# A fused graph-attention network on one core: the attention layers in another slot order, with V, the output projection and the low parts of keys moved

## The chip, the core and the metric

The kernel runs as one program on one core of a Trainium2 chip. The core has TensorE (PE, matrix products; its weight loads are shown as PEld), VectorE (DVE), ScalarE (ACT), GpSimd (POOL) and SyncE (SP), which issues all DMAs here. Each engine works through its own instructions in order; semaphores tie them together. The metric is the device time of one execution in microseconds (us), lower is better.

## What is computed

One graph layer (12 heads, gated) and three attention layers over 32 samples of 256 nodes with 384 features. Each layer ends in a layer norm. The change is in the attention layers only:

```python
def _L1_gnn_ref(seq_inputs, Wq, bq, Wk, bk, Wv, bv, Wf, bf, graph_mask):
    q = _heads(seq_inputs @ Wq + bq)      # 6 heads of 64
    k = _heads(seq_inputs @ Wk + bk)
    v = _heads(seq_inputs @ Wv + bv)
    scores = jnp.einsum('bhqd,bhkd->bhqk', q, k) / np.sqrt(HEAD_SIZE)
    bias = jnp.where(graph_mask, 0.0, NEG)[:, None]
    probs = jax.nn.softmax(scores + bias, axis=-1)
    ctx = jnp.einsum('bhqk,bhkd->bhqd', probs, v)
    ctx = ctx.transpose(0, 2, 1, 3).reshape(seq_inputs.shape[0], seq_inputs.shape[1], H)
    return ctx @ Wf + bf

x = _layernorm(x + _L1_gnn_ref(x, ..., adj), axis=-1)   # and so for L2, L3
```

## The kernel before

**Numbers in two parts.** Products in `float32r` are made of a high and a low part of each operand: `product` (L83 to L88) issues three matmuls, low by high, high by low and high by high. So each operand is split after it is made: ScalarE copies the high part out of the bank (`high_xt`, `high_qk`, `high_ct`), VectorE subtracts it and writes the low part (`low_xt`, `low_qk`, `low_ct`).

**Slots.** The order of work on every engine is written out by hand. The attention layers run sample by sample, 96 samples (32 in each of three layers), in slots; sample (half, u) is number 2 x half + u. In one slot, `nxt` is the sample whose x is transposed and projected, `cur` the one before it (scores, softmax) and `prev` the one before that (contexts, output projection). `every_slot_of_all_layers` calls each engine's `slot` in that order; `crossing` is the hand-written stretch in which the last sample of the graph layer and the first two of attention overlap.

**TensorE** in a slot: transposes of x (`transpose_x`, L1411), scores of heads 0 and 1, q and k of chunk 0 (`make_qk`; a chunk is 128 of 384 features, two heads), scores 2 and 3, chunk 1, contexts of `prev` (L1478), scores 4 and 5, V (`make_v`), chunk 2, output projection of `prev` (`make_back`). Three banks `pj` serve all projections in the turn of `BANK_ORDER`. The first transposes wait on `pj_read` until the last low parts of the sample before are read out of the bank.

**The stack.** For the scores, q and k of both heads of a chunk lie in `stack` with high and low parts in the two halves of the partitions. ScalarE writes one half (`own_rows`, L800), two DMAs per chunk copy the other half across partitions (`move`, L374). The low part of k lies in a tile of its own, `k_lo`, zero in the rows of the other head, and is written by two 64-row instructions (L1056).

**The way of the probabilities.** VectorE adds the mask and takes the maximum (`mask_and_max`, L1066), ScalarE the exponential (L807), VectorE the reciprocal of the sums for each pair of heads (`invert`, L1079), GpSimd multiplies (`normalise`, L579), VectorE transposes in blocks of 32 (`turn`, L1087), a DMA writes the pair to DRAM (`lay`, L381, 512 KB) and another reads it back with the blocks in place (`fetch`, L388); then TensorE makes the contexts. SyncE waits until a `lay` has landed before it issues its `fetch`. It also moves, loads the next x and adjacency (`load_again`), and stores results (`store`), all from one queue, in a fixed order.

**GpSimd** also makes the mask, adds the output bias to x (L557) and does the layer norm (L562 to L572).

## Time and profile before

| | |
|---|---|
| Median of 3 runs | 3052.48 us (3051.24 to 3055.53) |
| The profiled execution | 3051.53 us, span of the core 3049.7 us |
| Mean granted TensorE clock | 0.961 |
| Busy, share of the span | TensorE 91%, VectorE 85%, ScalarE 75%, GpSimd 59% |
| Graph layer | from the start to about 850 us |
| Attention layers | from about 850 us to the end |

A busy share is the time in which an engine had an instruction in work. Since TensorE's matmuls overlap (a row's duration is longer than the distance to the next start), starts are the better measure of its pace. The granted clock is a share of full speed, which is 2.4 GHz; the other level is 1.2 GHz. The waits of a DMA queue are SyncE's own waits before it can issue.

### The profile page before, as it was taken

To read this page: it belongs to the slowest core of one execution; us is meant where nothing else is said; L and a number is where in the kernel's file an instruction comes from. 1 tells how busy PE (TensorE), PEld (TensorE's weight loads), DVE (VectorE), ACT (ScalarE), POOL (GpSimd) and SP (SyncE) were. 2 spreads that over 40 slices of the span, in tenths; PEclk is the share of its full clock that TensorE was granted. 3 is DMA by queue.
4 is the path that set the end of the run, shared out by engine and by line. 5 is a ranking of instruction groups with operands and counts; after the bars stand their busy time and mean duration, and the time that the engine had idled before them with its cause. 6 is when DMAs were issued, how large, how long until landed. Compare 5 with 4: busy or idle time off the path is not lost. (4 is left out here: it accounts for less than half of the span.)

```text
span 3049.7 us, 67047 instructions
## 1 busy us (share of the span) xinstructions
PE 2771.7 (91%) x20128; PEld 2479.0 (81%) x20128; DVE 2587.4 (85%) x7497; ACT 2272.8 (75%) x6600; POOL 1809.7 (59%) x1550
## 2 busy tenths in 40 slices
PE   8999999999988899899898899899899898998996
PEld 7888888888877888888888888788888888888885
DVE  6999998998888888888888888888888888888885
ACT  7999999999966667666666666676666676666663
POOL 3777766666655566555555566555555555555554
PEclk9999999999999999999999999999999999999998
DMA  2111111111166666666667666666666666666664
GB/s 88 35 35 35 35 35 35 35 35 35 50 199 226 211 208 215 210 217 209 211 213 235 212 216 209 219 206 220 208 212 212 207 216 209 216 208 208 219 205 155
DMA packets 346726, 500.45 MB, mean 164 GB/s; under 512 B 58112, under 2 KB 272000, under 8 KB 345984
## 3 DMA queue, kind: packets, MB, share of 16 engines
q1 hardware_dynamic: 346368, 496.16, 50.2%
q8 instruction: 165, 2.70, 0.4%
q14 instruction: 193, 1.58, 0.2%
HBM read 219.24 MB, written 201.33 MB: 138 GB/s over the span
## 5 line engine op out<-in xcount | busy, mean ns | idle before, releaser
L579 POOL TENSOR_TENSOR probs<-probs,recs 128x1024 f32<-128x1024 f32 x288 | 545.5, 1894 | 461.7 <-DVE recs L1079 461.7
L1087 DVE STREAM_TRANSPOSE turned_sb<-probs 128x512 f32<-128x512 f32 x576 | 609.8, 1099 | 205.2 <-POOL probs L579 202.3
L807 ACT ACTIVATE probs<-logits,nmax 128x256 f32<-128x256 f32 x1152 | 572.4, 498 | 173.0 <-DVE nmax L1066 170.6
L86 PE MATMUL pj<-xt_hi,w_lo 128*128 128x256 f32 x1728 | 506.6, 293 | 12.6 <-issue 11.1
L87 PE MATMUL pj<-xt_lo,w_hi 128*128 128x256 f32 x1728 | 500.2, 289 | 0.0
L88 PE MATMUL pj<-xt_hi,w_hi 128*128 128x256 f32 x1728 | 498.1, 288 | 0.0
L1066 DVE CUSTOM_DVE_ANT_0 logits<-s,mask 128x256 f32<-128x256 f32 x1152 | 423.8, 420 | 73.5 <-PE s L1466 63.4
L557 POOL TENSOR_TENSOR residual<-x,br 128x384 f32<-128x384 f32 x192 | 190.0, 1011 | 426.7 <-DVE mix L1098 426.7
L678 ACT ACTIVATE g_exps<-g_v,g_nmax 128x256 f32<-128x256 f32 x768 | 385.2, 515 | 2.9 <-DVE g_nmax L972 0.6
L800 ACT ACTIVATE stack<-split 64x512 fp32r<-64x512 f32 x576 | 363.4, 631 | 12.4
L86 PEld LDWEIGHTS pj<-xt_hi,w_lo 128*128 128x128 f32 x1728 | 349.7, 202 | 20.3 <-issue 18.2
L785 ACT ACTIVATE xt_hi<-pj 128x384 fp32r<-128x384 f32 x192 | 94.4, 491 | 357.4 <-PE pj L1411 357.2
L792 ACT ACTIVATE split<-pj,bc 128x256 fp32r<-128x256 f32 x576 | 238.1, 464 | 164.0 <-PE pj L88 163.8
L87 PEld LDWEIGHTS pj<-xt_lo,w_hi 128*128 128x128 f32 x1728 | 345.1, 200 | 0.0
L1465 PE MATMUL s<-k_lo,stack 128*128 128x256 f32 x1152 | 341.6, 323 | 3.5 <-DVE nmax L1066 3.5
L88 PEld LDWEIGHTS pj<-xt_hi,w_hi 128*128 128x128 f32 x1728 | 342.5, 198 | 0.0
L572 POOL TENSOR_SCALAR out<-mix,mv,rstd 128x384 f32<-128x384 f32 x192 | 316.0, 1652 | 20.0 <-issue 19.4
L1466 PE MATMUL s<-stack 128*128 128x256 f32 x1152 | 324.1, 308 | 0.0
L972 DVE CUSTOM_DVE_ANT_0 g_v<-s,g_v 128x256 f32<-128x256 f32 x768 | 286.9, 420 | 35.9 <-ACT g_v L672 29.9
L1411 PE MATMUL pj<-identity,x 128*128 128x128 f32 x576 | 114.9, 316 | 202.3 <-DVE k_lo L1056 191.7
L1056 DVE SCALAR_TENSOR_TENSOR k_lo<-pj,bc,split 64x256 fp32r<-64x256 f32 x576 | 275.9, 479 | 4.1
L1465 PEld LDWEIGHTS s<-k_lo,stack 128*128 128x128 f32 x1152 | 245.0, 213 | 40.3 <-issue 36.5
(119 smaller groups left out, 7726.5 us busy)
## 6 DMA issues: line engine op xcount, KB each, us to landing
turned<-turned_sb SPq DMA_DIRECT2D x288, 512.0 KB, 4.0
pt_copy<-turned SPq DMA_DIRECT2D x288, 512.0 KB, 4.3
stack<-split SPq DMA_DIRECT2D x576, 128.0 KB, 2.6
y<-out SPq DMA_DIRECT2D x128, 384.0 KB, 4.7
x<-y SPq DMA_DIRECT2D x96, 384.0 KB, 4.2
x<-x SPq DMA_DIRECT2D x32, 384.0 KB, 3.1
adj<-adj SPq DMA_DIRECT2D x128, 64.0 KB, 4.1
w_whole<-att_w SPq DMA_DIRECT2D x3, 2304.0 KB, 11.4
```

Of the source, the lines that this page charges most:

```text
L86: pe.matmul(out, a[1], b[0], start=first, stop=False)
L87: pe.matmul(out, a[0], b[1], start=False, stop=False)
L88: return pe.matmul(out, a[0], b[0], start=False, stop=last)
L572: pool.tensor_scalar(out_sb[u][:, t, :], mix[:, t, :], mv[:, t, 0:1], rstd[:, t:t + 1], ALU.subtract, ALU.mult).then_inc(ln_done, 1)
L579: pool.tensor_tensor(probs[:, heads, :, :].rearrange("p h t n -> p (h t) n"), probs[:, heads, :, :].rearrange("p h t n -> p (h t) n"), rec ...
L678: last = act.activation(g_exps[:, h % 4, t, :], g_v_sb[:, h % 3, t, :], ACT.Exp, scale=-1.0, bias=g_nmax[:, u, h, t:t + 1], accum_out=g_su ...
L800: last = act.activation(stack[rows_of(s), c, s, :, :], f32(split_slot(u, c)[rows_of(s), K_HI:Q_HI + 1:2, :]), ACT.Identity)
L807: last = act.activation(probs[:, (HEADS * u + h) % 4, t, :], logits[:, h % 2, t, :], ACT.Exp, scale=-1.0, bias=nmax[:, u, h, t:t + 1], acc ...
L1066: last = dve.tensor_tensor_reduce(out=logits[:, h % 2, t, :], in0=s_ps[h % 2][:, t, :], in1=mask[u][:, t, :], scale=-HEAD_DIM ** -0.5, sca ...
L1087: last = dve.transpose(turned_sb[b][:, :, :].rearrange("p k (z h q) -> p k z h q", z=NT, h=2 * NT)[:, :, kt], probs[:, 2 * b:2 * b + 2, :, ...
L1465: pe.matmul(s_ps[s][:, t, :], queries, k_lo[:, c, s, :], start=True, stop=False)
L1466: last = pe.matmul(s_ps[s][:, t, :], queries, stack[:, c, s, STACK_K, :], start=False, stop=True)
```

## The change

The slots are called with up to four samples: `new` (transposes of x, q and k), `cur` (scores, softmax, and now V), `prev` (contexts) and `old` (now the output projection, residual, statistics and norm); SyncE also gets the one before `old`, whose result it stores. So V and the output projection come one slot later than before. The contexts move from the middle to the end of TensorE's slot. The third pair of `cur` is normalised, transposed, written and fetched in the slot after. Scores are issued head by head instead of in pairs, and each waits for the maximum two heads before.

The low part of k goes into the same tile as the others (`split`, now four wide) in one 128-row instruction, and ScalarE's copy (`own_rows`) takes it to the stack, which is three wide now; `k_lo` is gone. That copy now waits for the low parts (`pj_read`) instead of the high ones. The moves across partitions take q low and k high, two runs of 1 KB a row that no longer lie side by side in the source.

The banks are taken in another turn, and the waits of `make_v`, `make_back`, `make_qk` follow it. `crossing` is adapted (V of the second sample and the third transpose of the first fall into the slots). The diff, cut to its core; a line of "..." also stands where removed lines of the old slots, printed above, are left out:

```diff
...
+def every_slot_of_all_layers(slot, behind=3):
+
+
+    def sample(i):
+        return divmod(i, 2) if 0 <= i < LAYERS * B else None
+
+    for i in range(2, LAYERS * B + behind):
+        slot(*(sample(i - k) for k in range(behind + 1)))
...
-        stack = sb("stack", [P, DC, 2, 2, N], F32R)
-        k_lo = sb("k_lo", [P, DC, 2, N], F32R)
+        stack = sb("stack", [P, DC, 2, 3, N], F32R)
...
-        BANK_ORDER = ("x0", "x1", "qk0", "qk1", "v0", "v1", "qk2", "back0", "back1")
+        BANK_ORDER = ("v0", "x0", "v1", "x1", "back0", "back1", "qk0", "qk1", "qk2")
...
-        K_HI, Q_LO, Q_HI = range(3)
+        Q_LO, Q_HI, K_HI, K_LO = range(4)
...
-                    sp.dma_start(f32(stack[rows_of(1 - s), c, s, :, :]), f32(split_slot(u, c)[rows_of(s), K_HI:Q_LO + 1, :])).then_inc(moved[c], 16)
+                    sp.dma_start(f32(stack[rows_of(1 - s), c, s, STACK_Q:STACK_K + 1, :]), f32(split_slot(u, c)[rows_of(s), Q_LO:K_HI + 1:2, :])).then_inc(moved[c], 16)
...
+            def slot(new, cur, prev, old, stored):
+                if cur:
+                    move(*cur, 2)
+                if prev:
+                    fetch(*prev, 0)
+                    lay(*prev, 1)
+                    fetch(*prev, 1)
+                if stored:
+                    store(*stored)
+                elif prev == first:
+                    g_store(*g_odd)
+                if prev:
+                    lay(*prev, 2)
+                    fetch(*prev, 2)
+                if new:
+                    move(*new, 0)
+                if cur:
+                    load_again(*cur)
                     lay(*cur, 0)
...
+                if new:
+                    move(*new, 1)
...
+            def slot(new, cur, prev, old):
+                if prev:
+                    normalise(*prev, 2)
                 if cur:
                     normalise(*cur, 0)
                 if old:
                     inverse_std(*old, EPS)
+                if cur:
+                    add_output_bias(*cur, layer_of(cur[0]))
+                    normalise(*cur, 1)
+                if new:
+                    make_mask(*new, prev)
+                if old:
                     layer_norm(*old)
...
+                if new:
+                    part = 2 * (new[0] % HALVES) + new[1] - 8
+                    if 0 <= part < PARTS and layer_of(new[0]) + 1 < LAYERS:
+                        split_weights(layer_of(new[0]) + 1, part)
...
             def own_rows(half, u, c):
-                act.wait_ge(pj_hi, split_of(half, u, QK[c]))
+                act.wait_ge(pj_read, split_of(half, u, QK[c]))
                 act.wait_ge(scores, scored(half, u, c))
                 for s in range(2):
-                    last = act.activation(stack[rows_of(s), c, s, :, :], f32(split_slot(u, c)[rows_of(s), K_HI:Q_HI + 1:2, :]), ACT.Identity)
+                    last = act.activation(stack[rows_of(s), c, s, :, :], f32(split_slot(u, c)[rows_of(s), Q_HI:K_LO + 1, :]), ACT.Identity)
                 last.then_inc(owned, 1)
...
+            def slot(new, cur, prev, old):
+                if old:
+                    high_ct(*old, 1, layer_of(old[0]))
+                    high_ct(*old, 2, layer_of(old[0]))
+                if cur:
+                    own_rows(*cur, 1)
+                if new:
+                    high_xt(*new, 0)
+                if cur:
+                    copy_v(*cur, 0)
                     exp(*cur, 0)
+                    copy_v(*cur, 1)
                     exp(*cur, 1)
...
+                if new:
+                    high_xt(*new, 1)
+                if cur:
+                    own_rows(*cur, 2)
                     exp(*cur, 2)
+                if new:
+                    high_qk(*new, 0, layer_of(new[0]))
+                if cur:
                     exp(*cur, 3)
...
+                if new:
+                    own_rows(*new, 0)
+                    high_qk(*new, 1, layer_of(new[0]))
                 if cur:
                     exp(*cur, 4)
+                if new:
+                    high_qk(*new, 2, layer_of(new[0]))
+                if prev:
+                    high_ct(*prev, 0, layer_of(prev[0]))
+                if cur:
                     exp(*cur, 5)
...
             def low_qk(half, u, c, layer):
                 dve.wait_ge(pj_hi, split_of(half, u, QK[c]))
-                dve.wait_ge(scores, scored(half, u, c))
-                parts, ps = split_slot(u, c), bank(half, f"qk{c}")
-                dve.scalar_tensor_tensor(parts[:, Q_LO, :], ps[:, Q * N:(Q + 1) * N], bc[:, layer, Q, c:c + 1], f32(parts[:, Q_HI, :]), ALU.add, ALU.subtract)
-                for s in range(2):
-                    rows = rows_of(s)
-                    last = dve.scalar_tensor_tensor(k_lo[rows, c, s, :], ps[rows, K * N:(K + 1) * N], bc[rows, layer, K, c:c + 1],
-                                                    f32(parts[rows, K_HI, :]), ALU.add, ALU.subtract)
+                parts, ps = split_slot(u, c), bank(half, u, f"qk{c}")
+                for m, hi, lo in ((Q, Q_HI, Q_LO), (K, K_HI, K_LO)):
+                    last = dve.scalar_tensor_tensor(parts[:, lo, :], ps[:, m * N:(m + 1) * N], bc[:, layer, m, c:c + 1], f32(parts[:, hi, :]), ALU.add, ALU.subtract)
                 last.then_inc(pj_read, 1)
...
+            def slot(new, cur, prev, old):
+                if old:
+                    low_ct(*old, 1, layer_of(old[0]))
+                if cur:
+                    mask_and_max(*cur, 0)
+                if old:
+                    low_ct(*old, 2, layer_of(old[0]))
+                if new:
+                    low_xt(*new, 0)
+                if cur:
+                    mask_and_max(*cur, 1)
+                if prev:
+                    turn(*prev, 2)
+                if new:
+                    low_xt(*new, 1)
+                if cur:
+                    mask_and_max(*cur, 2)
+                    invert(*cur, 0)
+                if old:
+                    add_back(*old, 0)
+                if cur:
+                    mask_and_max(*cur, 3)
                 if old:
                     add_back(*old, 1)
...
                     statistics(*old)
...
+                if new:
+                    low_qk(*new, 0, layer_of(new[0]))
+                if cur:
+                    invert(*cur, 1)
+                    mask_and_max(*cur, 4)
                     turn(*cur, 0)
...
+                if new:
+                    low_qk(*new, 1, layer_of(new[0]))
+                if cur:
                     mask_and_max(*cur, 5)
...
                     turn(*cur, 1)
+                if new:
+                    low_qk(*new, 2, layer_of(new[0]))
+                if prev:
+                    low_ct(*prev, 0, layer_of(prev[0]))
+                if cur:
                     invert(*cur, 2)
...
+            def transpose_x(half, u, t):
+                if (half, u) == second:
+                    pe.wait_ge(v_read, at(NT, *first, NT))
+                    pe.wait_ge(pj_read, split_of(*first, QK[2]))
+                elif t == 0:
+                    pe.wait_ge(pj_read, split_of(half, u, QK[1]) - HI_STEPS)
+                elif half:
+                    pe.wait_ge(v_read, at(NT, half, u, 1 - NT))
...
+            def scores_of(half, u, h):
+
+                c, s = divmod(h, 2)
+                pe.wait_ge(maxed, at(HEADS, half, u, h - 1))
+                if s == 0:
+                    pe.wait_ge(pj_read, split_of(half, u, QK[c]))
+                    pe.wait_ge(owned, at(DC, half, u, c + 1))
+                    pe.wait_ge(moved[c], moves_of(half, u))
+                for t in range(NT):
+                    queries = stack[:, c, s, STACK_Q, t * P:(t + 1) * P]
+                    pe.matmul(s_ps[s][:, t, :], queries, stack[:, c, s, STACK_K_LO, :], start=True, stop=False)
+                    last = pe.matmul(s_ps[s][:, t, :], queries, stack[:, c, s, STACK_K, :], start=False, stop=True)
+                last.then_inc(scores, 1)
...
+            def slot(new, cur, prev, old):
+                if cur:
+                    scores_of(*cur, 0)
+                    make_v(*cur, 0, layer_of(cur[0]))
+                if new:
+                    transpose_x(*new, 0)
+                if cur:
+                    scores_of(*cur, 1)
+                    make_v(*cur, 1, layer_of(cur[0]))
+                    scores_of(*cur, 2)
+                if new:
+                    transpose_x(*new, 1)
+                if old:
+                    make_back(*old, 0, new, cur, layer_of(old[0]))
+                if cur:
+                    scores_of(*cur, 3)
+                if old:
+                    make_back(*old, 1, new, cur, layer_of(old[0]))
+                if new:
+                    make_qk(*new, 0, layer_of(new[0]))
+                if cur:
+                    scores_of(*cur, 4)
+                if new:
+                    make_qk(*new, 1, layer_of(new[0]))
+                if cur:
+                    scores_of(*cur, 5)
+                if new:
+                    make_qk(*new, 2, layer_of(new[0]))
+                if prev:
+                    for c in range(DC):
+                        pair_of_contexts(*prev, c)
```

SyncE, one slot in the middle of the attention layers. `turned` is the tile in DRAM, so a row `turned<-turned_sb` is a `lay` and `pt_copy<-turned` a `fetch`; `laid` and `fetched` count their landings. Before:

```order
L381 DMA turned<-turned_sb 128x1024 [waits turned,fetched0]
L374 DMA stack<-split 64x512 [waits pj_read,scores]
L374 DMA stack<-split 64x512
L388 DMA pt_copy<-turned 128x4x256 [waits laid0,contexts]
L355 DMA y<-out 128x2x384 [waits ln_done]
L381 DMA turned<-turned_sb 128x1024 [waits turned,fetched1]
L388 DMA pt_copy<-turned 128x4x256 [waits laid1,contexts]
L381 DMA turned<-turned_sb 128x1024 [waits turned,fetched2]
L374 DMA stack<-split 64x512 [waits pj_read,scores]
L374 DMA stack<-split 64x512
L388 DMA pt_copy<-turned 128x4x256 [waits laid0,contexts]
```

After:

```order
L373 DMA turned<-turned_sb 128x1024 [waits turned,fetched0]
L366 DMA stack<-split 64x2x256 [waits pj_read,scores]
L366 DMA stack<-split 64x2x256
L366 DMA stack<-split 64x2x256 [waits pj_read,scores]
L366 DMA stack<-split 64x2x256
L380 DMA pt_copy<-turned 128x4x256 [waits laid0,contexts]
L373 DMA turned<-turned_sb 128x1024 [waits turned,fetched1]
L380 DMA pt_copy<-turned 128x4x256 [waits laid1,contexts]
L344 DMA y<-out 128x2x384 [waits ln_done]
L373 DMA turned<-turned_sb 128x1024 [waits turned,fetched2]
L380 DMA pt_copy<-turned 128x4x256 [waits laid0,contexts]
```

Write 1 stood behind the store and now stands right behind fetch 0; the store has gone between fetch 1 and write 2. Two moves fill the time between write 0 and fetch 0, and none that between write 2 and fetch 2.

TensorE, from the end of one slot into the next. Before:

```order
L88 MATMUL pj<-w_hi,ct_hi 128x384
L1411 MATMUL pj<-identity,x 128x128 [waits x_loaded1,pj_read]
L1411 MATMUL pj<-identity,x 128x128 x2
L1411 MATMUL pj<-identity,x 128x128 [waits back_read,pj_read]
L1411 MATMUL pj<-identity,x 128x128 x2
L1465 MATMUL s<-k_lo,stack 128x256 [waits owned,moved0,pj_read,maxed]
L1466 MATMUL s<-stack 128x256
```

After, with the contexts last and the first V product behind the first head's scores:

```order
L1452 MATMUL pt<-pt_copy,v 64x256 [waits v_read,fetched1,ct_split]
L1452 MATMUL pt<-pt_copy,v 64x256 x3
L1452 MATMUL pt<-pt_copy,v 64x256 [waits v_read,fetched2,ct_split]
L1452 MATMUL pt<-pt_copy,v 64x256 x3
L1439 MATMUL s<-stack 128x256 [waits owned,moved0,pj_read,maxed]
L1440 MATMUL s<-stack 128x256
L1439 MATMUL s<-stack 128x256
L1440 MATMUL s<-stack 128x256
L76 MATMUL pj<-w_hi,xt_lo 128x384 [waits pj_read]
```

The slot began with the transposes, waiting on `pj_read`; it begins with scores now, and its last waits are those for the three fetches.

VectorE, the end of a slot and the start of the next. Before:

```order
L1087 STREAM_TRANSPOSE turned_sb<-probs 128x4x128 [waits laid1,normed]
L1087 STREAM_TRANSPOSE turned_sb<-probs 128x4x128
L1079 RECIPROCAL recs<-sums 128x4 [waits exped]
L1087 STREAM_TRANSPOSE turned_sb<-probs 128x4x128 [waits laid0,normed]
L1087 STREAM_TRANSPOSE turned_sb<-probs 128x4x128
L1053 SCALAR_TENSOR_TENSOR split<-pj,bc,split 128x256 [waits scores,pj_hi]
L1056 SCALAR_TENSOR_TENSOR k_lo<-pj,bc,split 64x256 x2
L1098 TENSOR_TENSOR mix<-pj,residual 128x384 [waits back_made,ln_done,x_biased] x2
```

After:

```order
L1056 STREAM_TRANSPOSE turned_sb<-probs 128x4x128 [waits laid0,normed]
L1056 STREAM_TRANSPOSE turned_sb<-probs 128x4x128
L1026 SCALAR_TENSOR_TENSOR split<-pj,bc,split 128x256 [waits pj_hi]
L1026 SCALAR_TENSOR_TENSOR split<-pj,bc,split 128x256
L1042 SCALAR_TENSOR_TENSOR ct_lo<-cx,bc,ct_hi 128x256 [waits ct_hi_done]
L1048 RECIPROCAL recs<-sums 128x4 [waits exped]
L1042 SCALAR_TENSOR_TENSOR ct_lo<-pt,bc,ct_hi 128x256 [waits ct_hi_done]
L1035 ISA logits,nmax<-s,mask 128x256 [waits exped,mask_ready,scores]
```

The third transpose (with its wait on `normed`) stood ahead of the last low parts of q and k; now the last low parts follow the second transpose, and the third comes in the next slot.

## Rows read from the trace of the kernel before

**Rows 1.** The page's first part: busy time and share of the span of each engine

```profile
PE 2771.7 (91%) x20128; PEld 2479.0 (81%) x20128; DVE 2587.4 (85%) x7497; ACT 2272.8 (75%) x6600; POOL 1809.7 (59%) x1550
```

**Rows 2.** Stretches: start:end, us, busy time by engine (instructions), clock, DMA share, GB/s

```profile
300.00:600.00 300.00, 293.62 (x2344) 253.82 (x2345) 271.12 (x891) 295.99 (x917) 209.94 (x197) 1.00 0.11 36
1200.00:2900.00 1700.00, 1532.42 (x10756) 1392.81 (x10755) 1441.62 (x3960) 1144.10 (x3211) 955.98 (x779) 0.95 0.66 213
```

**Rows 3.** Timeline of TensorE: start, duration, line, tiles, count, idle before; two slots' starts

```profile
856.33 1.08 PE L1411 MATMUL pj<-identity,x 128*128 128x128 f32 x4 [5.36 <-DVE k_lo L1056]
...
2979.32 0.55 PE L1411 MATMUL pj<-identity,x 128*128 128x128 f32 x3 [2.02 <-DVE k_lo L1056]
```

**Rows 4.** Waits from 1200 to 2900 us: us in all, times, longest

```profile
PE pj L1411 <- DVE k_lo L1056: 150.4, 75, 2.3
```

**Rows 5.** The same columns as rows 2, for three neighbouring slots

```profile
1204.40:1226.55 22.15, 19.73 (x145) 17.79 (x145) 19.25 (x54) 15.24 (x43) 14.02 (x12) 1.00 0.67 217
1226.55:1249.53 22.98, 20.96 (x145) 19.08 (x145) 19.35 (x54) 15.36 (x43) 14.00 (x12) 0.93 0.62 207
1249.53:1272.69 23.16, 21.01 (x144) 19.24 (x144) 19.34 (x54) 15.36 (x43) 14.00 (x12) 0.93 0.64 208
```

**Rows 6.** Timeline of TensorE in the slot that opens at 1204.40 us

```profile
1206.82 0.35 PE L86 MATMUL pj<-xt_hi,w_lo 128*128 128x256 f32 x1 [0.28 <-issue]
...
1224.19 0.34 PE L88 MATMUL pj<-w_hi,ct_hi 128*128 128x384 f32 x1
```

**Rows 7.** Timeline of VectorE near the end of a slot

```profile
1516.91 0.13 DVE L1079 RECIPROCAL recs<-sums 128x4 f32<-128x4 f32 x1
1519.16 2.08 DVE L1087 STREAM_TRANSPOSE turned_sb<-probs 128x512 f32<-128x512 f32 x2 [2.11 <-POOL probs L579]
...
1521.49 0.97 DVE L1056 SCALAR_TENSOR_TENSOR k_lo<-pj,bc,split 64x256 fp32r<-64x256 f32 x2
```

**Rows 8.** Groups by line and form over the whole span: count, busy us, mean ns

```profile
L800 ACT ACTIVATE stack<-split 64x512 fp32r<-64x512 f32 x576 | 363.4, 631 | 12.4
...
L1056 DVE SCALAR_TENSOR_TENSOR k_lo<-pj,bc,split 64x256 fp32r<-64x256 f32 x576 | 275.9, 479 | 4.1
...
L1053 DVE SCALAR_TENSOR_TENSOR split<-pj,bc,split 128x256 fp32r<-128x256 f32 x288 | 136.0, 472 | 5.0 <-ACT split L792 2.0
...
L708 ACT ACTIVATE g_ce<-g_ce 128x768 f32<-128x768 f32 x32 | 27.1, 846 | 1.4 <-DVE g_ce L951 1.4
```

**Rows 9.** Timeline of TensorE in the slot that opens at 1204.40 us: pace of its parts

```profile
1212.19 1.08 PE L1478 MATMUL cx<-pt_copy,v 128*64 128x256 f32 x8
...
1214.93 0.39 PE L1465 MATMUL s<-k_lo,stack 128*128 128x256 f32 x1
...
1219.10 0.28 PE L86 MATMUL pj<-xt_hi,w_lo 128*128 128x256 f32 x1
...
1221.22 0.34 PE L86 MATMUL pj<-w_hi,ct_lo 128*128 128x384 f32 x1
```

**Rows 10.** SyncE's own waits from 1200 to 2900 us

```profile
SPq L81 <- DMA turned<-turned_sb: 523.7, 193, 5.1
```

**Rows 11.** Timeline of SyncE's DMA issues: start, duration of the issue, line

```profile
1517.08 0.33 SPq L381 DMA_DIRECT2D turned<-turned_sb  x1
1521.09 0.36 SPq L388 DMA_DIRECT2D pt_copy<-turned  x1
1521.56 0.44 SPq L381 DMA_DIRECT2D turned<-turned_sb  x1
1522.63 1.18 SPq L374 DMA_DIRECT2D stack<-split  x2
1527.08 0.37 SPq L388 DMA_DIRECT2D pt_copy<-turned  x1
1527.56 0.44 SPq L350 DMA_DIRECT2D x<-y  x1
```

**Rows 12.** Landing times of the writes to DRAM (line 381), 1200 to 2900 us

```profile
DMA to landing us min/median/max: 2.6/4.0/7.7
```

More of the change, by code:

```diff
@@ L50, in g_every_slot, with layer_of @@
         slot((pair + 1, 0), (pair + 1, 1), (pair, 1))
[L53 to L75 removed]
+def every_slot_of_all_layers(slot, behind=3):
[3 more added lines that the diff above has]
+        slot(*(sample(i - k) for k in range(behind + 1)))
+def layer_of(half):
+    return half // HALVES
 def held(eng, sem, value, passed):
@@ L427, in _, with crossing @@
+                if new:
+                    move(*new, 1)
+                if new and new[1] and new[0] % HALVES == 2 and layer_of(new[0]) + 1 < LAYERS:
+                    load_weights(layer_of(new[0]) + 1)
+            def crossing():
+                for c in range(DC):
+                    move(*first, c)
+                load_again(*first)
+                g_store(*g_even)
+                move(*second, 0)
+                lay(*first, 0)
+                move(*second, 1)
             start(sp, *g_stored, *stored, *moved, *laid, *fetched)
@@ L460, in _ @@
             load(*second)
-            for layer in range(LAYERS):
-                samples_of_layer(layer)
-            end = LAYERS * HALVES - 1
-            lay(end, 1, 0)
-            fetch(end, 1, 0)
-            store(end - 1, HALVES - 2, 1)
-            lay(end, 1, 1)
-            fetch(end, 1, 1)
-            lay(end, 1, 2)
-            fetch(end, 1, 2)
-            store(end, HALVES - 1, 0)
-            store(end, HALVES - 1, 1)
+            crossing()
+            every_slot_of_all_layers(slot, behind=4)
             for u in range(2):
@@ L590, in split_weights @@
                 pool.tensor_tensor(lo, whole, f32(hi), ALU.subtract).then_inc(w_split, 1)
-            def slot(cur, nxt, prev, layers, opening=False, part=None):
-                old = before(prev)
+            def slot(new, cur, prev, old):
+                if prev:
+                    normalise(*prev, 2)
                 if cur:
@@ L630, in crossing @@
                 g_total(*g_odd)
-                normalise(*first, 2)
                 g_inverse_std(*g_odd, 4 * EPS)
@@ L651, in _ @@
             crossing()
-            every_slot_of_all_layers(pool, slot)
-            close(end_sample)
+            every_slot_of_all_layers(slot)
         @block.scalar
@@ L1106, in statistics @@
                     dve.bn_aggr(mv[:, t, :], stats[:, t, :]).then_inc(aggr, 1)
-            def slot(cur, nxt, prev, layers, opening=False, part=None):
-                _, nxt_layer, prev_layer = layers
-                old = before(prev)
+            def slot(new, cur, prev, old):
[20 more added lines that the diff above has]
+                    mask_and_max(*cur, 3)
@@ L1206, in crossing @@
                 low_qk(*second, 2, 0)
-                turn(*first, 2)
                 g_statistics(*g_odd)
@@ L1229, in _ @@
             crossing()
-            every_slot_of_all_layers(dve, slot)
-            close(end_sample)
+            every_slot_of_all_layers(slot)
         @block.tensor
```

271 lines of the change are left out of this document (62 added, 209 removed).

## Prediction

> **What bounds the kernel now.** Start with the page's first part (the span is 3049.7 us): TensorE busy 91%, VectorE 85%, ScalarE 75% [rows 1]. The medians over the span mix two stages, so the next view is the table by stretch. From 300 to 600 us (layer 0) TensorE is busy 97.9% at granted clock 1.00; from 1200 to 2900 us (the attention layers) it is busy 90% at 0.95, and the DMA share is 0.66 instead of 0.11 [rows 2]. The change touches the second stage only, so the question is how long one slot of it lasts. The six transposes of x open every slot: those of sample 2 start at 856.33 us, those of sample 95 at 2979.32 [rows 3]. That is 93 slots in 2122.99 us, 22.83 us each.
>
> Next, the waits of that stage. TensorE waits before those transposes, 75 times, 150.4 us in all, 2.0 us each, for the last low part of k (`k_lo`) [rows 4]. Three neighbouring slots show what one is made of [rows 5]: 22.15 us at clock 1.00, 22.98 and 23.16 us at 0.93. All three have the same 2.0 us wait, so a slot at full clock saves 0.8 to 1.0 us. In the first, which opens at 1204.40, the last matmul starts at 1224.19 and lasts 0.34 [rows 6]: 20.13 us. Of that, 0.28 is a stall before the q and k products [rows 6]. **TensorE's own work in a slot at full clock is thus about 19.85 us**, and the wait, the slow stretches and small stalls make up the other 3.0 of 22.83.
>
> Why is `k_lo` late? VectorE's own rows tell it [rows 7]: reciprocal at 1516.91, then 2.11 us idle for GpSimd's normalised probabilities, the transpose of the third pair (1519.16), and only then the low part of q and that of k (1521.49 to 1522.46), which TensorE waits for. VectorE waits for GpSimd, and TensorE waits for both.
>
> **The parts of the change.**
> *The low parts of k.* 288 instructions of 64x256 at 479 ns twice per chunk become one of 128x256; the q one of that shape takes 472 ns [rows 8]. VectorE saves 3 x 479 ns, 1.4 us a slot. It is busy 19.2 to 19.35 us of a slot [rows 5], so about 17.9 after. ScalarE's copy of own rows grows from 512 to 768 elements: 631 ns now; a 128x768 of layer 0 takes 846 [rows 8]. Bounds +0 (the width hidden by the overlap of neighbours) and +0.215; I take the upper, 6 x 0.215 = 1.3 us a slot. ScalarE goes from 15.3 to 16.6 us and stays below TensorE. The copy now waits for the low part as well; behind it are the next q, k copy and an exponential. TensorE's work is unchanged.
>
> *Third transpose in the next slot.* `turn(prev, 2)` goes behind the next slot's second maximum. GpSimd gets a whole slot start for its 1.9 us, so the 2.1 us idle goes. The next transposes of x no longer wait for the last low part but for the one of chunk 1, made some 4 us earlier. **The 2.0 us wait goes.** V, now one slot later, waits for the banks of chunks 0 and 2; the second of these is needed 2.9 us into the slot.
>
> *What is late next on the engines.* I lay the new slot out by starts of the full-clock slot [rows 9]: contexts 2.74 us, two scores and both V products 4.17 (so a score 0.5, a V product 1.56), a q, k chunk 2.12; a back product is as long as a V product, three transposes 0.45. TensorE's start at 0: score 0 and V to 2.1, x0 2.5, score 1 and V to 4.6, score 2 and x1 5.5, back 0 to 7.1, score 3 and back 1 to 9.2, qk0 to 11.4, score 4 and qk1 to 14.1, score 5 and qk2 to 16.8, contexts to 19.6, and with the changes between kinds of product 19.85. VectorE gets the x0 copy at 3.3, then maximum 1, third transpose to about 7.0, x1, maximum 2, back 0, maximum 3, back 1 (to 10.1), statistics to 11.5, qk0's low parts from 12.5 when ScalarE has its high parts, and from there without a wait 0.9 + 0.15 + 0.7 + 2.1 + 0.9 + 0.7 + 2.1 + 0.9 = 8.45 us to the last low parts at 20.95, which is 1.1 into the next slot. TensorE's waits are met with 1 us and more to spare: x1's low part at 7.6 for 9.2, chunk 2's at 1.1 for 3.0. The engines alone would give about 19.85 us a slot.
>
> *The DMA queue.* Every pair of heads goes out to DRAM and back, and SyncE waits for the write before it issues the read: 523.7 us of waits in 75 slots, 7 us a slot, its longest [rows 10]. Before, only write 2 stood right behind a fetch, with a move in its wait. After, the order is fetch 0, write 1, fetch 1, store, write 2, fetch 2, move, load, write 0, two moves. I price that ring from SyncE's starts [rows 11], from one fetch 2 to the next. Fetch 2 to the move 0.5, the move 1.2, x and adjacency 1.0, then write 0. A write issued alone comes back after 4.0 (1517.08 to 1521.09); one issued 0.5 us behind a fetch needs 5.5 (1521.56 to 1527.08), because its data queue behind the fetch's. Write 0 stands behind the load: between them, 5.0. Fetch 0 and the issue of write 1: 0.5. Write 1 stands right behind a fetch: 5.5. Fetch 1 and store: 1.05. Write 2 stands behind a fetch and a 384 KB store: 6.0. Sum 0.5 + 1.2 + 1.0 + 5.0 + 0.5 + 5.5 + 1.05 + 6.0 = **20.75 us a slot.** That is above the engines' 19.85: the wait removed comes back as one of about 1 us before the third pair's contexts (or at the q, k copy that waits for the move of chunk 0). Bounds of the three writes: all at the median of 4.0 [rows 12] gives 16.25 for the ring, which hides it behind TensorE (19.85); 5.5, 6.3 and 6.8 give 22.85. I keep the middle, since two of the writes stand where the 5.5 one stood.
> The moves carry the same bytes in runs of 1 KB instead of 2 KB: no row prices that; the DMA share of 0.66 [rows 2] on 22.8 us is 15 us of work, so even 1 us more leaves it below 20.7. Between 0 and +0.5 on the ring; I take 0.
>
> *Fill and drain.* The last sample still has three pairs written and fetched one after another; from 2979.32 to the end is 70.4 us. One more slot stands in the loop, but it is only back and norm, which `close` did. I take 0, bounds -5 and +5.
>
> **Sum.** 94 full slots x (22.83 - 20.75) = 195 us. The profiled execution took 3051.53 us, 0.95 below the median of 3052.48: 3051.5 - 195 = 2856. I say **2855 us.**
>
> **The rivals.**
> *A. TensorE alone.* The writes land near their median because bursts interleave better; the ring hides and a slot is 19.85. 94 x 2.98 = 280: about 2771. For it: clock 1.00 throughout layer 0 at 97.9% busy [rows 2] and the spare time above. Against it: the 5.5 us of a write behind a fetch.
> *B. The clock still falls.* The ring's wait of 1 us, or several shorter ones, keeps part of every slot at 1.2 GHz. In the rows a slow slot costs 0.8 to 1.0 us over a full-clock one [rows 5]; on top of 20.75 that is up to 21.7: 94 x 1.13 = 106, about 2945. For it: two slots in three fall now with a wait of 2.0 us. Against: in layer 0, with TensorE idle 2% of the time in many small pieces, it stays at 1.00 [rows 2]. The Trainium skill, TensorE: Matmul & The Clock Gate, section "A second HAM failure mode: psum-queue depth-cycling", says that idle moments between groups of matmuls, as a kernel cycles through its banks, can make the clock oscillate and cost throughput; the new order cuts TensorE's slot into sixteen pieces on three banks. By that rule this case is likelier; layer 0's clock [rows 2] disagrees.
> *C. Slower: the write queue saturates.* Place: writes 1 and 2 in the ring. If a write behind fetch and store lands after 7.7 us, the longest seen [rows 12], and so do all three, the ring is 20.75 + 2.7 + 2.2 + 1.7 = 27.35 and the kernel 94 x 4.5 = 425 us slower (3475); it decides from where the three together take over 18.6 us instead of 16.5. Just past it, say 8% over, is more likely than the full price. Against it: 5.5 was measured with two moves behind it as well.
> *D. Nothing.* The order view shows the waits moved as the diff says, so that TensorE's 2 us wait stays can only be if GpSimd's norm (3.3 us) at the slot's end holds up the third normalise by over 2 us; then 3050. Little speaks for it: GpSimd is busy 956 of 1700 us [rows 2].
>
> **How the numbers follow.** Forecast (ring, 20.2 to 21.2 us a slot, 2810 to 2905 us): 0.48. A: 0.25. B: 0.15. C: 0.07. D and small losses: 0.05. The range reaches down to A with a fill 5 us shorter and the stalls between products gone (19.6 a slot, 24 us), 2745, and up to B's end, 2945; C, D and the tails are left out. A measurement of this kernel can tell about 0.2% (6 us). Faster by more than that 0.89, within 0.03, slower 0.08.
>
> **What would show it.** Right: slots near 20.7 us; the wait for `k_lo` before the transposes of x gone; VectorE's instructions down by 288; SyncE's waits for the write above 7 us a slot, writes landing after 5 to 6 us, and the one TensorE wait of some size before the contexts (line 1452 of the new kernel), ended by a DMA or told as "issue". Wrong by A: no such wait, slots of 19.85, clock 1.00. Wrong by B: clock 0.93 in slots without a long wait. Wrong by C: median landing of `turned` near 7 us and a slot over 22.8. A wait of VectorE for ScalarE's copies above 1 us a slot would say that my layout of the engines was too kind.

## The result: 3030.7 us, a gain of 0.75% where 6.5% was forecast

The changed kernel takes 3030.69 us, median of 4 runs (3026.23 to 3033.22); the kernel before 3052.61 (3051.24 to 3055.53). The ratio is 0.9925 [0.9908, 0.9943]. The forecast was 2855, its range 2745 to 2945: the direction was right, the size was not, and the time lies outside the range. The profiled execution took 3031.44 us, its span is 3029.7.

**What went as said.** The page of the changed kernel, its first part, one group of part 5 and one of part 6:

```profile
PE 2752.4 (91%) x20128; PEld 2457.8 (81%) x20128; DVE 2437.9 (80%) x7209; ACT 2362.9 (78%) x6600; POOL 1805.6 (60%) x1550
...
L772 ACT ACTIVATE stack<-split 64x768 fp32r<-64x768 f32 x576 | 485.8, 843 | 3.4
...
turned<-turned_sb SPq DMA_DIRECT2D x288, 512.0 KB, 5.2
pt_copy<-turned SPq DMA_DIRECT2D x288, 512.0 KB, 4.5
stack<-split SPq DMA_DIRECT2D x576, 128.0 KB, 4.4
```

VectorE has 288 instructions fewer than in [rows 1], ScalarE's copy takes 843 ns (846 had been taken from a row of the same width, [rows 8]), and a write lands after a median of 5.2 us.

**What did not.** The waits of the changed kernel from 1200 to 2900 us (engine, line, releaser: us in all, times, longest), the engines' and then SyncE's own:

```profile
ACT split L764 <- issue: 320.8, 75, 9.0
DVE split L1026 <- ACT split L764: 254.0, 130, 4.8
...
PE pt L1452 <- issue: 145.6, 76, 5.9
```

```profile
SPq L71 <- DMA turned<-turned_sb: 762.6, 151, 9.5
SPq L71 <- DVE split L1026: 176.5, 75, 3.0
```

The wait for `k_lo` [rows 4] is gone. In its place TensorE waits 1.9 us a slot before the third pair's contexts (145.6 in 76), and two waits are there that the sum did not have: ScalarE 4.3 us a slot before its copies of q and k ("issue" means that the profile shows nothing that ended the wait), VectorE 3.4 us behind it.

The slots, by the first transposes of x of samples 2 and 95, in TensorE's timeline:

```profile
856.86 0.84 PE L1377 MATMUL pj<-identity,x 128*128 128x128 f32 x3
...
2956.87 0.61 PE L1377 MATMUL pj<-identity,x 128*128 128x128 f32 x3
```

That is 93 slots in 2100.01 us, 22.58 each, against 22.83 in [rows 3]: 23 us less, of which the tail gives back 2.4 (72.8 us from sample 95 to the end, 70.4 before). The forecast had 20.75 a slot. So 1.83 us a slot are to be explained. The attention stretch and four neighbouring slots (the columns of [rows 2]):

```profile
1200.00:2900.00 1700.00, 1531.76 (x10862) 1390.11 (x10862) 1337.92 (x3775) 1226.62 (x3248) 959.43 (x784) 0.96 0.70 215
...
1290.76:1312.64 21.88, 19.67 (x146) 17.65 (x144) 16.62 (x46) 15.12 (x40) 12.46 (x10) 1.00 0.67 207
1312.64:1336.60 23.96, 20.84 (x145) 18.74 (x145) 18.42 (x54) 16.92 (x46) 12.45 (x10) 0.93 0.66 208
1336.60:1357.55 20.95, 19.65 (x146) 17.62 (x145) 17.01 (x48) 15.59 (x42) 12.46 (x10) 1.00 0.70 221
1357.55:1380.48 22.93, 20.83 (x145) 18.91 (x145) 18.34 (x54) 16.85 (x46) 12.46 (x10) 0.93 0.70 214
```

The clock still falls (1.00 or 0.93), and the long slots are those at 0.93. That looks like rival B. It is tested below.

### The profile page after: what moved, and what is told of

Its sections match the earlier page's. It is cut to its first block and busy times, and to the rows that moved or that the text cites. A ratio compares the mean times of both kernels' runs of the same rounds, so it can differ in the third digit from the quotient of the medians.

```text
span 3029.7 us, 66563 instructions
## 1 busy us (share of the span) xinstructions
PE 2752.4 (91%) x20128; PEld 2457.8 (81%) x20128; DVE 2437.9 (80%) x7209; ACT 2362.9 (78%) x6600; POOL 1805.6 (60%) x1550
## 5 line engine op out<-in xcount | busy, mean ns | idle before, releaser
L1026 DVE SCALAR_TENSOR_TENSOR split<-pj,bc,split 128x256 fp32r<-128x256 f32 x576 | 248.3, 473 | 321.4 <-ACT split L764 318.8
L772 ACT ACTIVATE stack<-split 64x768 fp32r<-64x768 f32 x576 | 485.8, 843 | 3.4
L76 PE MATMUL pj<-xt_hi,w_lo 128*128 128x256 f32 x1728 | 483.3, 280 | 3.1 <-DVE xt_lo L1020 3.1
L77 PE MATMUL pj<-xt_lo,w_hi 128*128 128x256 f32 x1728 | 482.3, 279 | 0.0
L1452 PE MATMUL pt<-pt_copy,v 128*64 128x256 f32 x1536 | 220.3, 409 | 195.9 <-issue 193.8
L1439 PE MATMUL s<-stack 128*128 128x256 f32 x1152 | 332.2, 309 | 29.4 <-DMA stack<-split 26.2
L1452 PEld LDWEIGHTS pt<-pt_copy,v 128*64 128x64 f32 x1536 | 114.8, 143 | 277.1 <-issue 239.4
L76 PEld LDWEIGHTS pj<-xt_hi,w_lo 128*128 128x128 f32 x1728 | 325.2, 188 | 3.7 <-issue 3.7
L77 PEld LDWEIGHTS pj<-xt_lo,w_hi 128*128 128x128 f32 x1728 | 325.8, 189 | 0.0
L1440 PE MATMUL s<-stack 128*128 128x256 f32 x1152 | 312.1, 291 | 0.0
L1439 PEld LDWEIGHTS s<-stack 128*128 128x128 f32 x1152 | 226.5, 197 | 90.1 <-issue 87.7
L1440 PEld LDWEIGHTS s<-stack 128*128 128x128 f32 x1152 | 229.7, 199 | 0.0
```

Of the source, the lines that this page charges most:

```text
L76: pe.matmul(out, a[1], b[0], start=first, stop=False)
L77: pe.matmul(out, a[0], b[1], start=False, stop=False)
L772: last = act.activation(stack[rows_of(s), c, s, :, :], f32(split_slot(u, c)[rows_of(s), Q_HI:K_LO + 1, :]), ACT.Identity)
L1439: pe.matmul(s_ps[s][:, t, :], queries, stack[:, c, s, STACK_K_LO, :], start=True, stop=False)
L1440: last = pe.matmul(s_ps[s][:, t, :], queries, stack[:, c, s, STACK_K, :], start=False, stop=True)
L1452: last = pe.matmul(cx_banks[c][rows_of(s), :], v_sb[u][:, kt, h * HEAD_DIM:(h + 1) * HEAD_DIM], tokens(pt_sb[:, c, :, run]), start=kt == 0 ...
```

## Where the ring was priced too low

SyncE's starts in one slot of the changed kernel (366 is `move`, 373 `lay`, 380 `fetch`, 344 `store`):

```profile
1503.08 0.36 SPq L380 DMA_DIRECT2D pt_copy<-turned  x1
1503.62 1.25 SPq L366 DMA_DIRECT2D stack<-split  x2
1504.99 0.53 SPq L339 DMA_DIRECT2D x<-y  x1
...
1506.22 0.40 SPq L373 DMA_DIRECT2D turned<-turned_sb  x1
1506.82 5.73 SPq L366 DMA_DIRECT2D stack<-split  x4
1512.68 0.51 SPq L380 DMA_DIRECT2D pt_copy<-turned  x1
1513.31 0.47 SPq L373 DMA_DIRECT2D turned<-turned_sb  x1
1518.42 0.36 SPq L380 DMA_DIRECT2D pt_copy<-turned  x1
...
1519.44 0.40 SPq L373 DMA_DIRECT2D turned<-turned_sb  x1
1525.11 0.36 SPq L380 DMA_DIRECT2D pt_copy<-turned  x1
```

The order is the forecast's. From one start to the next, as means over 64 slots between 1200 and 2900 us with just this pattern of issues:

| piece | priced | measured |
|---|---|---|
| fetch 2 to move 0, move 0, x and adjacency to write 0 | 0.5 + 1.2 + 1.0 | 0.55 + 1.39 + 1.22 |
| **write 0 to fetch 0** | **5.0** | **0.61 + 5.84 = 6.45** |
| fetch 0 to write 1 | 0.5 | 0.64 |
| write 1 to fetch 1 | 5.5 | 5.15 |
| fetch 1 and store to write 2 | 1.05 | 1.06 |
| write 2 to fetch 2 | 6.0 | 6.00 |
| sum | 20.75 | 22.47 |

The writes behind a fetch were priced well. One piece is off by 1.45 us, and not by its landing: from issue to landing write 0 takes 5.2 us on the mean from 1200 to 2900 us, against 5.0 priced (all three writes 5.2 + 5.1 + 5.9 = 16.3, priced 16.5). The other 1.2 us is SyncE held up behind it: fetch 0 does not stand behind write 0 alone. Between them stand the moves of chunks 1 and 2 (the row of 5.73 us), and the move of chunk 2 waits for that chunk's low parts. ScalarE's and VectorE's timelines at the same time say why these are late:

```profile
1509.39 0.84 ACT L764 ACTIVATE split<-pj,bc 128x256 fp32r<-128x256 f32 x2 [4.89 <-issue]
```

```profile
1510.26 0.88 DVE L1026 SCALAR_TENSOR_TENSOR split<-pj,bc,split 128x256 fp32r<-128x256 f32 x2 [3.50 <-ACT split L764]
```

`split` has two buffers, and chunk 2 uses that of chunk 0. So `high_qk` of chunk 2 waits until the move of chunk 0 has landed (line 761). That move is issued 0.54 us behind fetch 2; ScalarE goes on 5.77 us after its issue. The second half of the move lands at 1509.32 us in the trace, and ScalarE starts at 1509.39. This closes a loop over ScalarE, VectorE and SyncE's queue, which makes the slot's length by itself: fetch 2 to move 0 0.54, to ScalarE's copy 5.77, to fetch 0 3.29 (high parts, low parts 1510.26 to 1511.14, the two moves), to write 1 0.63, to fetch 1 5.11, to write 2 1.02, to fetch 2 5.67: 22.03 us, the distance from 1503.08 to 1525.11. **Theory Q** is that this loop sets the slot. Rivals: **B** (**K** in the expectations), the fallen clock costs time of its own; **L**, the moves' runs of 1 KB land later than those of 2 KB; **S**, ScalarE's wider and later copy of own rows is what holds up its q, k copy.

## Experiments

All ratios compare with the kernel before, run beside them on the same chip (medians of 3052.6 to 3060.6 us), so gains between two runs of the table are taken from the ratios.

| | median us | ratio to before |
|---|---|---|
| changed kernel | 3030.69 | 0.9925 [0.9908, 0.9943] |
| e1, move of chunk 2 later | 2900.92 | 0.9476 [0.946, 0.9492] |
| e2, move of chunk 0 earlier | 2835.48 | 0.9268 [0.9252, 0.9285] |
| e3, both | 2812.18 | 0.919 [0.9176, 0.9204] |
| e7, both and the store moved | 2792.64 | 0.9152 [0.9126, 0.9178] |
| e4, runs of 2 KB | 3031.34 | 0.9912 [0.9898, 0.9927] |
| e5, old low parts | 3064.12 | 1.0035 [1.0018, 1.0051] |
| e6, e3 with old low parts | 2839.82 | 0.9298 [0.928, 0.9317] |
| b1, before with new low parts | 3335.42 | 1.0921 [1.09, 1.0942] |
| e8, long filler | 3266.16 | 1.0688 [1.067, 1.0706] |
| e9, shorter filler | 3053.85 | 0.9978 [0.9965, 0.9992] |

### e1: the move of chunk 2 no longer ahead of fetch 0

```diff
                 if prev:
                     fetch(*prev, 0)
                     lay(*prev, 1)
+                if cur:
+                    move(*cur, 2)
+                if prev:
                     fetch(*prev, 1)
```

(The move's lines ahead of fetch 0 are gone.)

> The changed kernel with one edit in SyncE's order: the move of chunk 2 stands behind fetch 0 and write 1 instead of ahead of fetch 0. Theory Q (the queue's ring is held by the move of chunk 2, which waits for the last low parts; write 0 to fetch 0 takes 6.45 us, of which the landing needs about 4.8): that piece falls to 4.8, the ring from 22.5 to about 20.9 us a slot, the kernel to about 2875. Rival L (the landings themselves are long, because the moves go in 1 KB runs): the bytes and runs are the same, so the slot falls by less than 0.3 us, above 3000. Rival K (TensorE's clock): the 3.5 us stretches at half clock stay, above 2980.

2900.92 us, 4.5% less than the changed kernel. The distance of write 0 and fetch 0 falls from 6.45 to 5.35 us (4.8 were expected; it is now the landing of write 0, still 5.2), write 1 to fetch 1 from 5.15 to 5.13 with the move in its wait, and the ring from 22.47 to 21.12 (20.9 expected). The granted clock is 1.00 from 1200 to 2700 us. ScalarE still waits 257.8 us in 79 slots, but SyncE's wait for VectorE's low parts, 176.5 us in the changed kernel, is gone:

```profile
SPq L71 <- DVE split L1027: 0.9, 3, 0.3
```

### e2: the move of chunk 0 ahead of fetch 2

```diff
                     lay(*prev, 2)
+                if new:
+                    move(*new, 0)
+                if prev:
                     fetch(*prev, 2)
-                if new:
-                    move(*new, 0)
```

> The changed kernel with one edit in SyncE's order: the move of chunk 0 of the new sample stands between write 2 and fetch 2 (in the wait for that write's landing) instead of behind fetch 2. Theory Q: the move's 1.4 us of issue leave the ring, it lands some 3 us earlier, so ScalarE's copy of chunk 2, the last low parts and the move of chunk 2 come earlier too and write 0 to fetch 0 falls from 6.45 to about 5. Ring 22.5 - 1.4 - 1.4 = 19.7, so TensorE's 19.85 and small waits bound it: 20.2 us a slot, about 2805. Rival L: less than 0.3 us a slot, above 3000. Rival K: above 2980.

2835.48 us (about 2805 were expected), the turn of the queue 20.25 us. Part 6 of its page, and ScalarE's wait for the moves from 1200 to 2900 us:

```profile
stack<-split SPq DMA_DIRECT2D x576, 128.0 KB, 3.0
...
ACT split L765 <- issue: 8.6, 8, 3.7
```

The moves land after a median of 3.0 us instead of 4.4 (those of chunk 0 alone, first and second: 2.6 and 2.8 instead of 4.3 and 4.8), and ScalarE's wait for them falls from 320.8 us to 8.6. The loop is cut at another place, with no byte less and no instruction less, and the gain is 6.6%, 201 us. Not all of it is the loop's: of the 2.2 us that the queue's turn loses, 1.0 is write 0 to fetch 0 (6.45 to 5.5), and some 1.4 is the issue of the two moves, which now lies in the wait for write 2; 0.2 comes back elsewhere. Two different edits that open the same loop both shorten that piece: theory Q holds.

### e3 and e7: both, and the store out of write 2's way

e3 has both edits. e7 moves the store from ahead of write 2 to behind write 0 as well:

```diff
-                if stored:
-                    store(*stored)
...
                 if prev:
                     lay(*prev, 2)
...
                     lay(*cur, 0)
+                if stored:
+                    store(*stored)
                 if new:
                     move(*new, 1)
```

> Both edits of SyncE's order. Theory Q: TensorE's own 19.85 us bound the slot already with the second edit alone, so this is 19.9 to 20.2 us a slot, 2775 to 2805, and within 1% of the second edit alone. If each edit took away a wait of its own, the two gains would add up to more. Rival L: above 3000. Rival K: above 2950.

> Both edits of the queue's order, and the store of the result from between fetch 1 and write 2 to behind write 0. Theory Q: write 2's landing loses the 384 KB ahead of it, fetch 2 is issued about 1 us earlier, and TensorE's 0.8 us wait before the third contexts goes: slot 20.0 to about 19.4 to 19.7, 2765 to 2800. Rival T (TensorE's own work bounds already): no change from 2812, within 0.3%.

2812.18 and 2792.64 us, both beat both kernels; e3 is above its 2775 to 2805 but within 1% of e2, e7 within its 2765 to 2800, with a longer slot than the 19.4 to 19.7 expected. From e3 to e7 the turn of the queue falls from 20.07 to 19.86 us: the store's 0.7 between fetch 1 and write 2 now lies in write 0's wait, and 0.5 comes back as longer waits for writes 1 and 2. In e7 the first transposes of samples 2 and 95 stand at

```profile
858.37 0.84 PE L1379 MATMUL pj<-identity,x 128*128 128x128 f32 x3
...
2721.46 0.49 PE L1379 MATMUL pj<-identity,x 128*128 128x128 f32 x3
```

20.03 us a slot, the median of the queue's turns being 19.7. The engines-alone layout of the prediction gave 19.85. Its stretch from 1200 to 2900 us and the waits in it:

```profile
1200.00:2900.00 1700.00, 1516.24 (x11254) 1391.44 (x11250) 1379.50 (x3922) 1276.88 (x3359) 1004.56 (x819) 0.99 0.68 225
```

```profile
DVE split L1028 <- ACT split L766: 83.4, 78, 1.1
...
PE pt L1454 <- issue: 54.3, 81, 4.6
```

The span ends at 2791.4 us, so the last 109 us of this stretch are empty. Up to 2700 us TensorE is busy 1449.35 us of 1500 at clock 1.00, so the slot is now near TensorE's own work. VectorE's wait is down from 3.4 to 1.1 us a slot, TensorE's from 1.9 to 0.7.

### e4: the moves in runs of 2 KB

`split` is made five wide, so that k high and q low lie side by side again; nothing else changes.

```diff
-        Q_LO, Q_HI, K_HI, K_LO = range(4)
+        K_HI, Q_LO, Q_HI, _, K_LO = range(5)
```

> The changed kernel with the tile of split parts five wide, in an order in which k high and q low lie side by side, so that each move goes in runs of 2 KB again as in the kernel before; the order of everything stays. Rival L (1 KB runs make the landings of the moves 4.4 instead of 2.6 us and hold the ring): landings of the moves back near 3, 1.4 us a slot less, about 2900. Theory Q (the moves land late because a fetch and a load are in front of them and beside them): at most 0.3 us a slot, 3003 to 3035. Rival K: no change.

3031.34 us, moves landing after a median of 4.5 us instead of 4.4: rival L falls. The "0, at most 0.5 us" of the prediction for that was 0.

### e5 and e6: the low parts as before

Two 64-row instructions write k's low part straight into the stack, ScalarE copies 512 elements, and VectorE waits again for the scores of the sample before ahead of them (that line is left out below). e5 does it in the changed kernel, e6 in e3.

```diff
-                for m, hi, lo in ((Q, Q_HI, Q_LO), (K, K_HI, K_LO)):
-                    last = dve.scalar_tensor_tensor(parts[:, lo, :], ...)
+                dve.scalar_tensor_tensor(parts[:, Q_LO, :], ...)
+                for s in range(2):
+                    last = dve.scalar_tensor_tensor(stack[rows_of(s), c, s, STACK_K_LO, :], ...)
```

> The changed kernel with the low parts of k made as before: two 64-row instructions that write the stack directly, and ScalarE's copy of own rows 512 wide. Everything else, the queue's order too, stays. Theory Q: the low parts of chunk 2 are a link of the loop move 0, ScalarE, VectorE, move 2, fetch 0; the link grows by 0.5 us, so the slot does: about 3075. Rival S (ScalarE's wider copies, +0.2 us each, six a slot, are what ate the gain): 1.3 us a slot less, about 2910.

> Both edits of the queue's order and the low parts of k as before. Where the queue no longer bounds, VectorE has 1.4 us a slot more, 19.4 instead of 17.9, beside TensorE's 19.85. Theory Q: the new instruction is worth little while VectorE has spare time; the slot grows by 0 to 0.6 us over both edits alone (2812): 2812 to 2870. Rival S: it falls, below 2800.

3064.12 and 2839.82 us. Without the wide copy, ScalarE's wait stays (308.9 us in 75 slots in e5): rival S falls. In both orders the new low parts are worth 1.1% (0.9925 against 1.0035, 0.919 against 0.9298), some 0.36 us a slot, of the 1.4 us that they take off VectorE.

### b1: the low parts alone, in the old order

The kernel before with the new `split`, the three-wide stack and the copy that waits for the low parts; order and banks as before.

> The kernel before with only the low parts of k as in the change (one 128-row instruction a chunk, own rows 768 wide and waiting for the low parts, moves in 1 KB runs), in the old order of slots. VectorE has 1.4 us a slot less, of it 0.5 directly ahead of TensorE's 2.0 us wait; if nothing else moved, 0.5 us a slot, about 3005. Against it ScalarE, which made its copy right behind the high parts, now waits for VectorE twice a slot with exponentials behind it (2 us at chunk 0, more at chunk 1). I expect that this wins: slot 24 to 25.5 us, 3150 to 3300. Rival: the copy's wait is hidden, 2990 to 3050.

3335.42 us, 9.2% slower, more than the 3150 to 3300 expected. Its waits from 1200 to 2900 us, and the three copies of one slot in ScalarE's timeline:

```profile
ACT stack L799 <- DVE split L1053: 478.4, 198, 4.2
```

```profile
1503.31 1.69 ACT L799 ACTIVATE stack<-split 64x768 fp32r<-64x768 f32 x2 [4.12 <-DVE split L1053]
...
1514.00 1.70 ACT L799 ACTIVATE stack<-split 64x768 fp32r<-64x768 f32 x2 [2.27 <-DVE split L1053]
...
1519.47 1.70 ACT L799 ACTIVATE stack<-split 64x768 fp32r<-64x768 f32 x2 [0.94 <-DVE split L1053]
```

The copy, and the exponentials behind it, now wait for VectorE at every chunk, 7.2 us in each of the 66 slots. The longest of the three is that of chunk 2: its low parts stand behind VectorE's third transpose, which waits for GpSimd. The same edit gains 1.1% in the new order.

### e8 and e9: matmuls in TensorE's idle time

Extra products (v by v, overwritten by the contexts) ahead of the wait for the third pair's fetch. e8 has 14 in one half of the bank's rows, e9 has 8 that alternate between the halves:

```diff
                 pe.wait_ge(v_read, at(NT, half, u, NT))
+                if c == DC - 1:
+                    for i in range(8):
+                        pe.matmul(cx_banks[c][rows_of(i % 2), :], v_sb[u][:, 0, 0:HEAD_DIM], v_sb[u][:, 1, 0:N], start=True, stop=True)
                 pe.wait_ge(fetched[c], fetches(half, u))
```

> The changed kernel with 14 extra matmuls (v by v, 256 columns, some 0.13 us apart, 1.9 us) that TensorE makes before it waits for the third pair's fetch; the contexts overwrite their result. It fills the idle time of about 2 us there and changes nothing that SyncE, ScalarE or VectorE wait for, so the granted clock should stay at 1.00. In seven neighbouring slots of the changed kernel the three at full clock last 20.95 to 21.88 us (mean 21.5), the four at 0.93 last 22.93 to 23.96 (23.4). If the fallen clock is a cause of its own (the loss is loop plus clock), all slots become 21.5: 93 x (22.6 - 21.5) = 100 us less, about 2930. If the clock only follows the wait and the queue's loop sets every slot, the time stays within 0.5% of 3030. If the filler itself stands in the way where no wait is, it is up to 1.9 us a slot slower in some slots, and over 3030.

3266.16 us. It doesn't tell the theories apart: the filler was mis-sized. A row of it reads

```profile
1502.87 5.99 PE L1449 MATMUL pt<-v 128*64 128x256 f32 x27
```

It took 6 us instead of 1.9 (a product shows as two records), and TensorE was busy for the whole 1700 us.

> As the run with the filler before, where each of the 14 matmuls took 0.43 us (6 us in all, more than the idle time, so that TensorE itself set a slot of 25.1 us), but with 8 matmuls that alternate between the two halves of the bank's rows, as the contexts do, whose 4 take 1.08 us: some 2.1 us. The idle time before the third pair's contexts is 2.5 us in the changed kernel. If the fallen clock is a cause of its own, about 2930 (slots of 21.5 us, as the full-clock ones of the changed kernel); if it only follows the wait and the queue's loop sets every slot, within 0.5% of 3030; a mixture lies between. Slots where the fetch has landed early are up to 2 us longer, which would work against the first.

3053.85 us, 0.5% more than the changed kernel in the ratios. The stretch and a slot's filler:

```profile
1200.00:2900.00 1700.00, 1609.67 (x11973) 1422.73 (x11970) 1330.82 (x3743) 1218.97 (x3221) 955.18 (x780) 0.99 0.70 213
```

```profile
1516.63 1.90 PE L1449 MATMUL pt<-v 128*64 128x256 f32 x16
1519.71 1.08 PE L1455 MATMUL pt<-pt_copy,v 128*64 128x256 f32 x8 [1.18 <-DMA pt_copy<-turned]
```

The clock is at 0.99, and the ring is 22.64 us as before. **With the clock back, nothing is won; so the fallen clock is a companion of the long wait and not a cause of the time.** The filler itself does not hide a gain: in 62 of the 75 slots the third contexts still start within 0.1 us of the landing of their fetch, and in the other 13 it holds them up by 12 us in all, 0.2 us a slot, where B asks for 1.1 back. That delay is of the size of the 0.5%. Rival B falls, and the loop is left.

## Why the prediction was wrong, step by step

**Right.** The wait for `k_lo` goes; the price of the low parts on both engines (ScalarE busy 16.3 us a slot of the changed kernel, 16.6 priced); no cost of the short runs; the DMA queue as the next bound, with its order; the writes behind a fetch (5.15 and 6.00 for 5.5 and 6.0); fill and drain (2.4 us in the bounds of 5). The engines alone at 19.85 us: e7 reaches 20.03. And with the loop opened by e1 the ring is 21.12 us for 20.75 and the time, 2900.92 us, lies in the forecast's range: what the ring's sum lacked is in the main the loop.

**Wrong: the term "write 0 to fetch 0, 5.0".** It was priced as a landing, with the moves in its wait taken as free. A queue in order is also held up by whatever its other entries wait for, and one of them, the move of chunk 2, waits for VectorE, which waits for ScalarE, which waits for the move of chunk 0, issued right behind a 512 KB fetch. The prediction named that wait in half a sentence ("or at the q, k copy that waits for the move of chunk 0") and gave it no price, and it laid out VectorE's q and k work "from there without a wait" on the assumption that ScalarE's high parts are there. Its own last falsifier, a VectorE wait above 1 us a slot, is what came: 3.4. The row of the term measured 6.45, 1.45 of the 1.72 missing in the ring's mean; 0.46 and 0.14 more are the issues around it, and 0.35 came back at write 1. That SyncE waits for low parts stood in the waits of the kernel before, from 1200 to 2900 us, and no term was made of it:

```profile
SPq L81 <- DVE k_lo L1056: 301.1, 201, 4.2
```

**Left without a term: how long a move takes to land.** The page of before has

```profile
stack<-split SPq DMA_DIRECT2D x576, 128.0 KB, 2.6
```

This median mixes places. In the kernel before the two moves behind fetch 1 and write 2 land after 4.4 and 4.5 us on the mean, all others after 2.4 to 2.9. In the changed kernel the two of chunk 0 need 4.3 and 4.8, and ScalarE goes on 5.77 us after the issue of the first. In e2, where they need 2.6 and 2.8, write 0 to fetch 0 is 5.5 us instead of 6.45. What shares the queue with a small transfer was not asked for moves, though it was for writes.

**Rivals.** A (2771) is where e7 comes near (2792.64); C did not come, the three landings are 17.6 us with all that stands in them. B would have said 2945 at most and its mechanism does nothing here. D's figure (3050) is the nearest, but its mechanism is not what came: the wait for `k_lo` is gone, and another of the same size took its place. The case that did come, a wait closed over three engines, had no chance of its own, so the range was too narrow on the high side. The Trainium skill, TensorE: Matmul & The Clock Gate, section "A second HAM failure mode: psum-queue depth-cycling", warns of idle moments between groups as a kernel cycles through its banks; with the same sixteen pieces (nine of them on the three banks; the prediction puts all sixteen there) e1 and e7 have a clock of 1.00 from 1200 to 2700 us, so the pieces and banks alone do not bring the clock down here.

**What stays open.** e1 to e3 change the order, and with it when every transfer meets every other; how the 7.35% (225 us) between the changed kernel and e3 are made up was not measured apart. The landings of the three writes are 15.9 us a slot in e3 for 16.3, so shorter landings of writes are at most 0.3 us of the 2.4 that the queue's turn loses.

## What to carry to other kernels

Where one queue issues everything in order, price each entry by what it waits for, not only by how long it takes, and follow that wait until it ends or comes back to the same queue: a loop can set the pace though no engine in it is busy for more than 80% of the span, as here. Try small transfers that someone waits for ahead of large ones (e2), and entries that wait for an engine behind those that others wait for (e1). Before a slower clock is called a cause, fill the idle time and see whether the time falls.

## What was not expected of the hardware

- A 128 KB move between partitions lands, on the mean over the slots from 1200 to 2900 us, after 2.4 to 3.0 us where the last 512 KB fetch was issued 4.5 us or more ahead of it, and after 4.3 to 5.0 where one was issued within 4 us (kernel before, changed kernel, e1 and e2; the moves of chunk 0 need 4.3 and 4.8 in the changed kernel, 2.6 and 2.8 in e2). Runs of 1 KB and 2 KB make little difference (medians 4.4 and 4.5).
- Products of 64 output rows that alternate between the two halves of a bank's rows take 0.24 us each (8 in 1.90), those that stay in one half 0.43 (14 in 6 us).
- Clock 0.93 goes with longer slots: 0.8 to 1.0 us in the kernel before [rows 5], about 2 in the four slots of the changed kernel shown above. Yet 1.9 us of filler brought it back to 0.99 and left the time where it was.
